# Centring rows in the attention layers by a product with a constant matrix, and a table that gives each step its place in its engine's order

## The reference

```python
# L0 attention part, 4096 tokens, in 4 batches of 1024
attn = linear_attention(x)
x = layer_norm(x + attn); x = layer_norm(x + gated_ffn(x))
# L0 experts: all 8 experts on every token, added up
acc = sum((silu(x @ Wg[e]) * (x @ Wu[e])) @ Wd[e] for e in range(8))
# L1 attention part: 4 layers
for i in range(4):
    h = layernorm(x, ln1_w[i], ln1_b[i])          # (x - mean) / sqrt(var + eps)
    x = x + quaternion_spectral_attention(h)
    h = layernorm(x, ln2_w[i], ln2_b[i])
    x = x + gelu(h @ fc_w[i] + fc_b[i]) @ mproj_w[i] + mproj_b[i]
# L1 experts: each token goes to the 2 of 8 experts that bid most
```

## Time and profile before

| what | value |
|---|---|
| median of the runs | 1503.81 us |
| the profiled execution: its time is its span | 1503.8 us |
| TensorE busy | 1395.6 us (93%) |
| VectorE busy | 1250.3 us (83%) |
| ScalarE busy | 1042.7 us (69%) |
| GpSimd busy | 360.9 us (24%) |
| TensorE's mean granted clock | 0.981 |
| DMA, mean | 158 GB/s |
| chain that ended last | PE 44%, issue 20%, DVE 16%, ACT 9%, POOL 8%, DMA 2% |

### The profile page before, as it was taken

The page is one execution under the profiler, slowest core; times in us unless marked ns, Lnnn a source line. Parts: engine busy times, 40 slices in busy tenths (PEclk is TensorE's granted clock), DMA queues, the critical chain, the costliest instruction groups (busy, mean ns, idle before and its releaser), DMA issues.

```text
span 1503.8 us, 20880 instructions
## 1 busy us (share of the span) xinstructions
PE 1395.6 (93%) x6198; PEld 990.6 (66%) x6198; DVE 1250.3 (83%) x1511; ACT 1042.7 (69%) x2411; POOL 360.9 (24%) x251
## 2 busy tenths in 40 slices
PE   6999999999899999899999899999889999999858
PEld 4677766666566666566665667656677677777636
DVE  3344467877999989999959897999999999999996
ACT  6455757676886777766877768777857787776652
POOL 0001203110221402011131411131543353344410
PEclk9999999999999999999999999999999999999989
DMA  7763445335544554533363335355555556555244
GB/s 270 261 255 139 157 146 185 118 114 168 167 135 148 179 164 135 206 117 111 109 216 113 99 107 168 121 155 174 162 184 167 158 176 198 162 174 160 86 112 155
DMA packets 111243, 238.02 MB, mean 158 GB/s; under 512 B 13207, under 2 KB 52844, under 8 KB 109644
## 3 DMA queue, kind: packets, MB, share of 16 engines
q1 hardware_dynamic: 106588, 227.31, 47.9%
q0 software_dynamic: 4544, 9.38, 1.8%
HBM read 185.59 MB, written 43.86 MB: 153 GB/s over the span
## 4 chain that ended last, share of the span: by engine, by line
PE 44%; issue 20%; DVE 16%; ACT 9%; POOL 8%; DMA 2%; SPq 0%; ACTq 0%; POOLq 0%; DVEq 0%
PE bank L1363 8%; PE bank L1351 7%; PE bank L1353 6%; PE bank L1352 6%; POOL RSTD L1025 4%; PE bank L1543 3%; DVE AM L1087 3%; POOL ytok L1040 3%; ACT ROWS L865 2%; PE bank L1458 2%; DVE SH L1217 2%; DVE TA L1083 2%; PE bank L1452 1%; ACT ROWS L878 1%; DVE TA L1092 1%
## 5 line engine op out<-in xcount | busy, mean ns | idle before, releaser
L1025 POOL TENSOR_TENSOR RSTD<-SS,power_half 128x4 f32<-128x4 f32 x96 | 158.8, 1654 | 816.7 <-ACT ROWS L865 816.5
L1363 PE MATMUL bank<-SH,WD 128*128 128x512 f32 x512 | 263.6, 596 | 0.8 <-DVE X L1233 0.8
L1351 PE MATMUL bank<-NH,GU 128*128 128x512 f32 x512 | 245.5, 479 | 2.0 <-DMA GU<-halves 1.0
L1217 DVE TENSOR_TENSOR SH<-SH,bank 128x512 f32<-128x512 f32 x256 | 172.4, 682 | 76.4 <-ACT SH L853 46.4
L1087 DVE TENSOR_TENSOR AM<-AM,TA 128x1024 f32<-128x1024 f32 x192 | 230.2, 1219 | 0.9
L1083 DVE TENSOR_TENSOR TA<-QKV 128x2048 f32<-128x2048 f32 x96 | 219.5, 2287 | 1.2
L1353 PE MATMUL bank<-NL,GU 128*128 128x512 f32 x512 | 203.0, 397 | 0.0
L1352 PE MATMUL bank<-NH,GU 128*128 128x512 f32 x512 | 202.6, 396 | 0.0
L853 ACT ACTIVATE SH<-bank 128x512 f32<-128x512 f32 x256 | 153.1, 605 | 59.6 <-PE bank L1353 57.5
L878 ACT ACTIVATE ROWS<-bank,RSTD 128x128 f32<-128x128 f32 x384 | 110.0, 374 | 56.2 <-POOL RSTD L1025 50.8
L1578 PE MATMUL bank<-XT,GU 128*128 128x256 f32 x624 | 147.5, 381 | 0.3 <-DVE SH L1335 0.3
(11 more groups left out here) (232 smaller groups left out, 2764.8 us busy)
## 6 DMA issues: line engine op xcount, KB each, us to landing
GU<-halves SPq DMA_DIRECT2D x112, 512.0 KB, 4.2
QKV<-QKV SPq DMA_DIRECT2D x32, 720.0 KB
GU<-in_w_gu SPq DMA_DIRECT2D x39, 512.0 KB, 3.6
xg<-in_c_fill SPq DMA_DIRECT2D x8, 2080.0 KB
WD<-in_w_d SPq DMA_DIRECT2D x128, 128.0 KB, 2.2
FC<-ready_w SPq DMA_DIRECT2D x32, 512.0 KB, 5.2
WQ<-ready_w SPq DMA_DIRECT2D x32, 384.0 KB, 4.8
WD<-in_w_d SPq DMA_DIRECT2D x39, 256.0 KB, 3.8
```

Source lines behind the costliest of these rows:

```text
L1025: pool.tensor_tensor(RSTD[:], SS[:], (power_one if k[0] == "at" else power_half)[:], ALU.pow).then_inc(power_done, 1)
L1217: dve.tensor_tensor(SH[:, g % 4, :], SH[:, g % 4, :], banks[2 + g % 2][:], ALU.mult).then_inc(h_ready, 1)
L1351: pe.matmul(out, w_hi, x_hi, start=True, stop=False)
L1363: pe.matmul(banks[4][:], WD1[:, slot, :], SH[:, g % 4, :], start=first, stop=last).then_inc(down_done, 1)
```

## The change

In the norms `A` and `C` TensorE multiplies by `centre` as in the other norms. VectorE's step `centre`, its two instructions, the tiles `SUMS` and `SHIFT`, the semaphore `shift_set` and ScalarE's wait on it go. The planner and its numbers go too. In their place a table `PLACES` gives, for each step and engine, the place of each occurrence in that engine's order.

```diff
-class Plan:
-    ...
-TUNE = {
-    "early": 162.28,
-    ...
+PLACES = {
+    ...
+    "turn": {
+        "PE": (
+            1, 26, 64, 119, 230, 285, 386, 463, 44, 57, 150, 164, 325, 401, 517, 528, 51, 69, 156, 187, 350, 435, 523, 553, 75,
+    ...
 def schedule():
-    ...
-    return plan.run()
+
+    every, at = step_keys(), {}
+    for name, engines in PLACES.items():
+        for engine, places in engines.items():
+            mine = [key for key in every[name] if TAKES_PART.get((name, engine), lambda key: True)(key)]
+            assert len(mine) == len(places), (name, engine, len(mine), len(places))
+            for key, place in zip(mine, places):
+                at.setdefault(engine, {})[place] = (name, key)
+    orders = {engine: [steps[i] for i in sorted(steps)] for engine, steps in at.items()}
     ...
-    sums_before = count_before("ACT", ("keys_exp", "query"), lambda name, key: name == "scale" and key[0] == "at")
+    sums_before = count_before("DVE", ("keys_exp", "query"), lambda name, key: name == "normed" and key[0] == "at")
     ...
             elif name == "centre" and k[0] != "at":
                 act.wait_ge(centred, n + 1)
                 act.wait_ge(power_done, n)
-                if k in mean_no:
-                    act.wait_ge(shift_set, mean_no[k])
                 for i in range(GROUPS):
-                    shift = SHIFT[:, i:i + 1] if k in mean_no else root_eps[:]
-                    ins = act.activation(ROWS[:, i, :], LNB[:, i * P:(i + 1) * P], ACT.Square, bias=shift, scale=P ** -0.5,
+                    ins = act.activation(ROWS[:, i, :], LNB[:, i * P:(i + 1) * P], ACT.Square, bias=root_eps[:], scale=P ** -0.5,
                                          accum_out=SS[:, i:i + 1])
     ...
-            elif name == "centre":
-                dve.wait_ge(centred, n + 1)
-                dve.wait_ge(squared, n)
-                link(dve.tensor_reduce(SUMS[:], LNB[:].rearrange("p (g n) -> p g n", g=GROUPS), AX.X, ALU.add))
-                dve.tensor_scalar(SHIFT[:], SUMS[:], -float(P) ** -1.5, (EPS / P) ** 0.5, ALU.mult, ALU.add).then_inc(shift_set, 1)
     ...
                     for i in range(GROUPS):
-                        if k in mean_no:
-                            mm = pe.transpose(LNB[:, i * P:(i + 1) * P], src[:, i * P:(i + 1) * P], ident[:])
-                        else:
-                            mm = pe.matmul(LNB[:, i * P:(i + 1) * P], src[:, i * P:(i + 1) * P], centre[:], start=True, stop=True)
+                        mm = pe.matmul(LNB[:, i * P:(i + 1) * P], src[:, i * P:(i + 1) * P], centre[:], start=True, stop=True)
```

More of the change, by code:

```diff
@@ L161 @@
-TUNE = {
-    "early": 162.28,
[L163 to L171, removed]
-    "norm3": (-152.11, -101.28),
-    "start": (-234.15, -59.77),
-    "layer": -56.81,
-    "each": (529.64, -179.53, 37.96, 155.32, -140.7, -301.83, -32.74, -2.6, -193.3, -290.59, -294.68, -435.64, -289.05, -302.63, -221.2, 26.9, 222.94, -348.25, -561.95, -68.96, 29.66, 18.73, -170.57, 155.29, 279.8, -473.5, 244.77, -442.52, 365.61, -357.82, 326.43, 160.76),
-    "tile": (-240.56, -435.7, 140.4, 178.21, 65.79, 124.81, -81.13, -458.63),
-    "late": 137.91,
-    "pace": 3.53,
-    "prep": (-339.41, -474.98, -151.03, -846.55),
-}
@@ new lines, in schedule @@
+def schedule():
+    every, at = step_keys(), {}
[6 more added lines that the diff above has]
+    orders = {engine: [steps[i] for i in sorted(steps)] for engine, steps in at.items()}
+    assert all(sorted(steps) == list(range(len(steps))) for steps in at.values())
+    keys = {}
+    for name, engines in PLACES.items():
+        per_engine = [[key for n, key in orders[engine] if n == name] for engine in engines]
+        longest = max(per_engine, key=len)
+        if name == "normed":
+            longest = keys["turn"]
+        elif name == "route":
+            longest = [(t, i) for t, last in longest if last == 3 for i in range(4)]
+        assert all([key for key in longest if key in some] == some for some in per_engine), name
+        keys[name] = longest
+    halves, half_of = list(range(HALVES)), {}
+    freed = [key[0:2] for name, key in orders["DVE"] if name == "ham" and key[2] == HAM + 1]
+    for i, key in enumerate(key[0:2] for name, key in orders["ACT"] if name == "views" and key[2] == 0):
+        half_of[key] = i if i < HALVES else half_of[freed[i - HALVES]]
+    return orders, keys, half_of
@@ L427, in program @@
     SS, RSTD = sb("SS", [P, GROUPS]), sb("RSTD", [P, GROUPS])
-    SUMS, SHIFT = sb("SUMS", [P, GROUPS]), sb("SHIFT", [P, GROUPS])
     ROWS = sb("ROWS", [P, GROUPS, P])
@@ L545, in program @@
     xs_hi = sem("xs_hi")
-    shift_set = sem("shift_set")
     prep_kept = [sem(f"prep_kept{i}") for i in range(2)]
@@ L606, in program @@
         nth[(kind,) + tuple(key)] = seen[f] = seen.get(f, 0) + 1
-    token_means = [x for x in scalings if x[0] in ("A", "C")]
-    mean_no = {x: i + 1 for i, x in enumerate(token_means)}
     in_xs = [x for x in scalings if x[0] in ("A", "C")]
```

554 lines of the change are left out of this document (372 added, 182 removed), and 124 rows, old and new, of the table PLACES.

## The result

The changed kernel takes 1529.63 us (median of 4 runs, 1524.96 to 1535.53), the kernel before 1504.67 us beside it (4 runs, 1503.05 to 1507.08). The ratio is 1.016, 95% interval 1.0134 to 1.0186: slower by some 24 us, where 14 us faster was forecast. The time lies above the range and above the fullest form of the slower rival. Each run of the changed kernel lies 1.8 to 1.9 us above its span (the profiled one is 1530.54 us for a span of 1528.6), so the span before, 1503.8 us, belongs to a run of about 1505.6, and that it equals the median there is chance.

A forecast was written before the change was run, and what follows sets the result against it. TensorE and VectorE were taken to bound the kernel together, each losing time waiting for the other. From 1503.8 us, -8.2 for the centring and -6 for the order gave 1489.6, stated as 1490 us, range 1472 to 1509.

The forecast's parts named there:

- slower rival: TensorE becomes the bound and the products are paid: 1527 us in full, 1513 in the milder, likelier form; chance 0.15.
- The product: Centring on TensorE by product instead of four transposes: +0.45 us at each of 29 norms on the chain, +13.1 us.
- The sums: VectorE's row-sum pair removed at 20 places on the chain: -6.3, -5.7 and -9.3 us, together -21.3 us.
- the six places where the squares waited: Sums that held up ScalarE's squares behind `ham` steps: 1.55 us gained at each, -9.3 us; lower bound 0.81 each.
- Centring by itself: Product and removed sums together, in the norms: 13.1 - 21.3 = -8.2 us.
- The order: Moved steps on the engines and queues: -1.5 in the tail, -0.5 for a fill, -4 for the rest; -6 us.
- The gain of the other engines' new order: Some 450 other moved steps, not priced singly: -4 us, between 0 and about -13.
- The fill that moves: Fill of tile 5, thought ahead of expert weights asked for at 370.39, goes past six visits: 0 to 1.05 us, taken 0.5.
- The last `down` in the 4.28 us stop: In the tail, TensorE's last `down` of 2.82 us moves into a stop at 1433.63; gain taken as 1.5 us.
- `back` at nothing: Moving `back` behind the last `mproj` adds about 1.8 us to TensorE's list, mostly hidden by VectorE; taken as 0.
- POOL's order at nothing: Inverse roots go ahead of stores on POOL; 88 times a root found POOL idle, so taken as 0.
- The signs: Profile after: VectorE 55 us less busy, TensorE up to 28.8 more; squares' wait down some 30, turn-back stops 25 or less.

The follow-up runs named there:

- e2: Kernel before, old order, with the product in place of the transposes but VectorE's row sums and ScalarE's wait kept; 1519.98 us, ratio 1.0092.
- e3: Kernel before, old order, transposes kept, row sums and the wait on them removed, so the mean is left out; 1490.37 us, ratio 0.9887.
- e1: Kernel before, old order on every engine, with the product and without the row sums; 1508.66 us, ratio 1.0008.
- e9: Changed kernel with 32 loads and rolls and the fills of tiles 1 and 3 moved back earlier in SyncE's list alone; 1509.34 us, ratio 1.001.
- e4: Changed kernel with only SyncE's eight fills put back directly behind the visits of before; 1521.72 us, ratio 1.0105.

## Why the prediction was wrong, step by step

- **The product, +13.1 us:** right. `e2` gives +13.9 (10.6 to 17.3); with the sums gone the same exchange costs 18 in the old order and 16 in the new. An estimate by the factor 4 that the Trainium skill, "TensorE: Matmul & The Clock Gate", Terms, states was 38 us; the runs don't agree with it.
- **The sums, -21.3 us:** right in mechanism, too large. Taken out with transposes kept they gave 17.0 (`e3`, 14 to 20), and beside the product 12.7 (`e1` less `e2`, 0.0084 x 1508). With the lower bound of 0.81 us at the six places where the squares waited, in place of 1.55, the sum would have been 16.9, near what `e3` measured; that it was this term isn't shown.
- **Centring by itself, -8.2 us:** +1.2 us (`e1`, -0.9 to +3.3). Some 4 of the 9 us between them are the sums' size, 1 the product's, and 4 are what the pair gives less than its halves (13.9 - 17.0 = -3.1). The two terms were counted on the same chain and added; that TensorE's share of the chain is 64% in `e1` and 44% before would fit sums that are worth less once the product is in. But these last 4 us are not clear of the noise of three ratios, and the reason isn't shown.
- **The order, -6 us:** the step that failed. It cost about 23 us (1.016 less 1.0008). The sentence "The other fills and the loads on SP that move have landed long before they are needed; they cost nothing while their queue is not late" was wrong: 22 of the 23 us come back when 34 of these steps go back (`e9`). Two fills side by side delay one 128 KB load to 29.39 us, and steps that pass one to five visits come late, since visits are what SyncE waits at. The same paragraph had seen that a late load costs a wait, but took it as "like those 1.05 us", and the waits were 3.38, 4.23 and 9.44; the last paragraph named the case that would make the prediction wrong, and I gave it no chance and no rival.
- **The gain of the other engines' new order, -4 us:** not there. `e9` has it on all four, and is at 1.001 where the old order (`e1`) is at 1.0008.
- **The fill that moves, -0.5 us:** a misreading. The fill ahead of the weights of 370.39 is SyncE's fifth and stands behind visit 52: it is tile 4's and not tile 5's, and the change doesn't move it. In the changed kernel the weights behind it, asked for at 376.31, took 14.1 us, much as before.
- **The last `down` in the 4.28 us stop, -1.5 us, and `back` at nothing:** not borne out. The new tail of `e9` loses about 6 us by the table and 3 by the run times, which is not clear of noise; which of the moved steps does it wasn't tried alone.
- **POOL's order at nothing:** consistent with `e9`, where POOL has the new order and the loss is gone.
- **The signs:** the counts of instructions and TensorE's busy time came as stated; VectorE's busy time fell by 44 us and not by 55. The squares' wait fell only with the old order (82 to 55.7), not in the changed kernel (79.0); the stops at the turns back fell to 29.1 and not to 25.
- **The slower rival (1508 to 1527):** its time was near, its mechanism wasn't: products not given back cost 1.2 us, not 23.

What stays open: how the 22 us of SyncE's steps divide between fills and loads. `e4` says 8 for the fills, but it loses 3.14 us at 376 by the fill of tile 4 that it puts ahead of a load, so their share may be larger; and at the third jump a late load and a fill act together. Open too are the "remote" stops.

## What to carry to other kernels

When an order changes on several engines, read the queue that issues the loads first, not last: for each load that moves, look up when the waiting issues leave that it now stands behind (here five visits took 29.5 us), and compare with the time from its landing to its use. A large transfer without a hurry belongs behind the small loads that are needed soon (the same columns took 6.3 us ahead of a fill and 15.3 behind it, others 7.1 and 18.4), and two of them together delay what is behind both (29.4 us against 19.5). When a change removes one thing and adds another on the same chain, measure the pair too: here the halves made -3.1 us and the pair +1.2, and the forecast for the pair was -8.2.

## What the runs showed that was not expected

- A load of 128 KB, whose median from issue to landing over the kernel is 2.1 us, took 29.39 us behind two DRAM-to-DRAM fills of 2080 KB and the loads beside them, and 19.5 with one fill ahead.
- TensorE's granted clock was 0.50 behind stops of 3.38, 7.02 and 9.44 us, for 4 us at least each time.
- The two transfers of a roll (720 KB in a row of the page) left at 459.29 and 460.26 and let VectorE start at 468.44, 8 us after the second was issued.
- With product and no sums, the same instructions in other places of the lists took from 0.9991 to 1.0494 of the time before (1506.75 to 1580.96 us).
